# Raw scores in pairs, a stage's last values one step later, and three small VectorE steps in other forms

## The reference

```python
x = L0_attn_x                                   # 8 x 256 x 256, fp32
xn = _layernorm(x, axis=-1)
s = _L0_attn_ref(xn, ...)                       # latent attention, 16 heads, rotary part
g = _silu(_L0_ffn_ref(xn, ...))                 # attention block, then experts
x = x + s * g
...
# latent attention
c_q = x @ w_dq.T;  c_kv = x @ w_dkv.T
q = concat([c_q @ w_uq.T, rope(c_q @ w_qr.T)])  # per head 16 + 64
k = concat([c_kv @ w_uk.T, rope(x @ w_kr.T)])
out = softmax(q k^T * SCALE + causal mask) v;   s = out @ w_out.T
...
# the other branch
xn = _rmsnorm(x, w_ln1);  h = causal_attention(xn, 16 heads of 16)
x = residual + h @ Wo.T;  xn = _rmsnorm(x, w_ln2)
logits = xn @ Wr.T;  top 2 of 8 experts, softmax of the two
y = sum over experts of weight * (silu(Wg x) * (Wu x)) @ Wd
```

## Time and profile before

| what | us |
|---|---|
| median of 3 runs (809.0 to 813.9) | 810.94 |
| profiled execution | 808.98 |
| its span | 807.2 |
| TensorE busy in the span | 726.7 (90%) |
| VectorE busy | 551.0 (68%) |
| ScalarE busy | 429.0 (53%) |
| GpSimd busy | 387.9 (48%) |

### The profile page before, as it was taken

The page is one execution under the profiler, slowest core; times in us unless marked ns, Lnnn a source line. Parts: engine busy times, 40 slices in busy tenths (PEclk is TensorE's granted clock), DMA queues, the critical chain, the costliest instruction groups (busy, mean ns, idle before and its releaser), DMA issues.

```text
span 807.2 us, 17047 instructions
## 1 busy us (share of the span) xinstructions
PE 726.7 (90%) x5968; PEld 651.0 (81%) x5968; DVE 551.0 (68%) x1925; ACT 429.0 (53%) x895; POOL 387.9 (48%) x489
## 2 busy tenths in 40 slices
PE   4869999999999999999999999894799999999970
PEld 3858978978988987887888887572699999999970
DVE  3876567687587586586586596425488888888844
ACT  2434364365365365355355445451487777887752
POOL 3642452354453453463563464253455666556640
PEclk9978999999999999999999999777799999999995
DMA  9492663573473474384284186431889999999736
GB/s 293 109 177 48 92 152 74 78 163 77 64 159 83 64 151 103 50 161 107 40 159 107 43 159 160 140 104 30 234 204 240 230 230 229 262 275 254 170 36 217
DMA packets 81416, 115.54 MB, mean 143 GB/s; under 512 B 17475, under 2 KB 57667, under 8 KB 81283
## 3 DMA queue, kind: packets, MB, share of 16 engines
q1 hardware_dynamic: 70612, 101.74, 53.0%
q0 software_dynamic: 9856, 12.13, 8.5%
q10 hardware_dynamic: 864, 0.60, 0.3%
HBM read 70.06 MB, written 23.46 MB: 116 GB/s over the span
## 4 chain that ended last, share of the span: by engine, by line
PE 69%; DVE 12%; DMA 6%; issue 4%; ACT 4%; SPq 4%; POOL 2%; DVEq 0%; POOLq 0%; ACTq 0%
PE ps L703 63%; DVE ex L1572 2%; ACT ex L1299 2%; DVE stg L1571 2%; DVE ps L1631 2%; DMA qt<-stg 2%; PE ps L739 2%; SPq L446 2%; PE ps L1097 1%; DVE ps L1628 1%; DMA ln<-in_w_ln 1%; POOL stg L607 1%; PE ps L748 1%; SPq L458 1%; SPq L402 1%
## 5 line engine op out<-in xcount | busy, mean ns | idle before, releaser
L647 POOL TENSOR_SCALAR_AFFINE_SELECT ex<-ex 128x256 f32<-128x256 f32 x256 | 102.9, 407 | 169.8 <-ACT ex L1299 157.7
L1299 ACT ACTIVATE ex<-ps 128x384 f32<-128x384 f32 x240 | 115.8, 490 | 122.3 <-PE ps L703 118.5
L703 PE MATMUL ps<-qt,kt 81*128 81x128 f32 (+2 forms) x768 | 165.5, 330 | 4.2 <-issue 2.0
L1628 DVE CUSTOM_DVE_ANT_0 ps<-ps,mask 128x128 f32<-128x128 f32 x256 | 78.1, 305 | 74.3 <-PE ps L703 72.6
L703 PEld LDWEIGHTS ps<-qt,kt 81*128 81x128 f32 (+1 forms) x768 | 111.1, 197 | 15.8 <-issue 7.9
L607 POOL TENSOR_TENSOR stg<-stg,ex 128x512 f32<-128x512 f32 x64 | 82.5, 1291 | 80.2 <-DVE ex L1572 78.3
L1631 DVE CUSTOM_DVE_ANT_0 ps<-ps,mask 128x256 f32<-128x256 f32 x256 | 119.1, 465 | 0.0
L690 POOL DMA_INDIRECT expert_rows<-yo,slot_of x46 | 75.4, 1639 | 82.6 <-ACT yo L1419 63.1
L1456 DVE TENSOR_TENSOR wel<-raw,weh 128x768 fp32r<-128x768 f32 x92 | 87.7, 956 | 18.3 <-ACT weh L1150 18.3
L703 PE MATMUL ps<-xth,wh 128*128 128x256 f32 x384 | 78.9, 286 | 2.0 <-issue 2.0
L1571 DVE TENSOR_TENSOR stg<-ps,cos_t 128x512 f32<-128x512 f32 x64 | 44.1, 689 | 52.8 <-PE ps L703 45.8
(11 more groups left out here) (157 smaller groups left out, 1682.1 us busy)
## 6 DMA issues: line engine op xcount, KB each, us to landing
raw<-in_w_experts SPq DMA_DIRECT2D x92, 384.0 KB, 4.5
qt<-stg SPq DMA_DIRECT2D x64, 128.0 KB, 4.0
kt<-stg SPq DMA_DIRECT2D x64, 128.0 KB, 3.8
multi_heads<-stg SPq DMA_DIRECT2D x64, 128.0 KB, 2.4
qt<-multi_heads SPq DMA_DIRECT2D x32, 192.0 KB, 3.6
kt<-multi_heads SPq DMA_DIRECT2D x32, 128.0 KB, 3.4
qt<-stg SPq DMA_DIRECT2D x8, 256.0 KB, 4.6
kt<-stg SPq DMA_DIRECT2D x8, 256.0 KB, 6.1
```

The lines of the kernel that those rows point to most:

```text
L647: nc.gpsimd.affine_select(a, a, [[0, 2], [1, P]], ALU.is_ge, zero, 0, -1).then_inc(exm, 1)
L703: return nc.tensor.matmul(o, a, m, start=start, stop=stop, skip_group_check=True, **k)
L1299: nc.scalar.activation(ex[:, h % (2 * G), :], ps[4 + h % 2][:, P:4 * P], ACT.Exp, scale=scale).then_inc(ex_, 1)
L1628: nc.vector.tensor_tensor_reduce(out=o[:, 0:P], in0=o[:, 0:P], in1=mask2[:, 1, :], scale=-1.0, scalar=-2.0 * BIG, op0=ALU.add, op1=ALU.min ...
```

## The change

It has four parts. In T1 the raw heads are issued two at a time: heads h+1 and h+2 behind transposed head h, for h = 1, 3, ... 13, and none behind even heads. In T2 likewise: (4, 5) behind head 1, (6, 7) behind 3, (8, 9) behind 5, (10, 11) behind 7, (12, 13) behind 10, (14, 15) behind 12. T2's `values(3)` moves behind the next batch's first two raw heads, in the last batch too. Three small VectorE steps become two-tensor instructions that read the same tensor twice and take the larger of two equal numbers or of x + c and x.

```diff
@@ heads
-                    if h in ahead:
-                        max_head(ahead[h])
+                    for n in ahead.get(h, ()):
+                        max_head(n)
@@ stage_t1
-                             {h: h + 2 for h in range(H - 2)}, lambda: None, after)
+                             {h: (h + 1, h + 2) for h in range(1, H - 2, 2)}, lambda: None, after)
@@ stage_t2
-                ahead = {h: h + EARLY for h in range(8)} | {h: h + 3 for h in range(9, 13)}
-                heads(b, scores, st2, ex2, exm2, pv2, ov2, v2, before_h0, lambda: wait(pe, sd, b + 1), max_head, ahead,
-                      lambda: max_t1(b + 1), after)()
+                ahead = {h: (h + 3, h + 4) for h in range(1, 8, 2)} | {10: (12, 13), 12: (14, 15)}
+                return heads(b, scores, st2, ex2, exm2, pv2, ov2, v2, before_h0, lambda: wait(pe, sd, b + 1), max_head,
+                             ahead, lambda: max_t1(b + 1), after)
@@ batch (in the last batch alike)
                     max2(b)(0)
                     max2(b)(1)
                     if not first:
+                        values_before()
                         to_tokens()
...
-                    stage_t2(b, max1(b + 1), {2: project, 5: lambda: project_v2(b + 1)})
+                    return stage_t2(b, max1(b + 1), {2: project, 5: lambda: project_v2(b + 1)})
@@ stepped, plus_one, both
-                    nc.vector.tensor_scalar(step[:, :, :], step[:, :, :], 2.0 * P, None, ALU.add).then_inc(gst, 1)
+                    nc.vector.scalar_tensor_tensor(out=step[:, :, :], in0=step[:, :, :], scalar=2.0 * P, in1=step[:, :, :],
+                                                   op0=ALU.add, op1=ALU.max).then_inc(gst, 1)
-                    nc.vector.tensor_scalar(gsum[:, :], gexp[:, :], 1.0, None, ALU.add).then_inc(gst, 1)
+                    nc.vector.scalar_tensor_tensor(out=gsum[:, :], in0=gexp[:, :], scalar=1.0, in1=gexp[:, :],
+                                                   op0=ALU.add, op1=ALU.max).then_inc(gst, 1)
-                    copy(g[:, :, 0], gsum[:, :])
+                    nc.vector.tensor_tensor(g[:, :, 0], gsum[:, :], gsum[:, :], ALU.max)
```

More of the change, by code:

```diff
@@ L987, in p1_with_m1, with batch @@
                 stage_p1(b, after | {"mk": lambda: (head(0), head(1)), "q3": lambda: head(2), "k3": lambda: head(3)})
-            def batch(b, first, more):
+            def batch(b, first, more, values_before):
                 to_tokens = None
@@ L1081, in _ @@
             pe.wait_ge(s_c, 16 * 4)
-            batch(0, True, True)
+            values_left = batch(0, True, True, None)
             pe.wait_ge(wrd, 1)
             for b in range(1, last):
-                batch(b, False, True)
-            batch(last, False, False)
+                values_left = batch(b, False, True, values_left)
+            batch(last, False, False, values_left)
             def rows_transpose(blk):
```

## The result

The changed kernel takes 823.64 us (median of 4, 821.07 to 826.88), the kernel before 812.29 beside it: a ratio of 1.016 (95% interval 1.0129 to 1.0192), which is +13.0 us (10.5 to 15.6); the two medians by themselves are 11.4 apart. The forecast was +8.0 us, slower. The direction was right, the size was too small, and the median lies 0.14 us above the stated range.

What follows compares the result with a forecast made beforehand. The prediction took TensorE, busy 90% of the span, as what to watch, with its waits priced by stretch. T1's pairs 3.0, T2's boundaries 5.0 and small steps 0 made +8.0 us on 810.94: 818.9 us, range 806.0 to 823.5.

Steps and rivals of the forecast that it cites:

- Pairs in T1, first wait: T1, raw head 9: waits for maximum 7, which starts behind `kept`; `values(0)` 0.5 us later.
- Pairs in T1, the sum: T1, batches 1 to 6: six times 0.5 = +3.0 us; bounds 0 to 0.9 each, the upper if another pair waits.
- Pairs in T2: End of T2: `max_t1` and `values(2)` 0.50 us later behind maximum 15; nothing carried from the front.
- Values later: Batch boundary: mask wait hidden, ScalarE's copy uncovered, loads early enough; `to_tokens` +0.72 us including `max_t1`'s +0.50, seven boundaries +5.0.
- Small steps: P1 on VectorE: GpSimd holds the new two-tensor forms like the old ones; 0 us.
- The rival's price: P1: new forms escape GpSimd's hold, gaining 0.13 to 1.30 us each, -0.8 to -7.8 over six; chance 0.14, other gains over 4 us included.
- The sum: Whole kernel: 3.0 + 5.0 + 0 = +8.0 us, median 818.9 us.
- The range: Whole kernel: 806.0 to 823.5 us; upper end from T1 at 0.8 and a boundary at 1.1, 12.5 us in all.

Runs made afterwards that it cites:

- e14: Kernel before with T1's pairs alone, plus GpSimd's four scatters moved from behind masks 8 to 11 to behind 12 to 15; ratio 1.0075.
- e7: Kernel before with T1's pairs alone, plus VectorE's scaling moved from behind maximum 10 to behind 11; T1 21.92 us against 21.50, no ratio.
- e11: Kernel before with T2's pairs for raw heads 4 to 11 alone, raw heads 12 to 15 single where they were; ratio 1.0025.
- e1_small: Kernel before with the three small VectorE steps alone in their two-tensor forms; ratio 1.001.
- e6: Kernel before with L1747 cut into eight one-column instructions and P1's copy into two of one element; ratio 1.001 in its second run.
- e12_t1_spread: Kernel before with T1's pairs alone, plus `kept` moved behind maximum 7, statistics behind 9, scaling behind 11; ratio 1.0004.
- e13_no_hold: Kernel before with the small steps cut into one-element pieces, and the product of the two gates cut as well; ratio 1.0009.

## Why the prediction was right and wrong

- **Pairs in T1, first wait: right.** Forecast +0.5 behind `kept`; `values(0)` came at 10.81 against 10.31, with 0.25 of idle TensorE and a fresh weight load at raw head 9.
- **Pairs in T1, the sum: wrong, and this is the step that failed most.** "I take 0.5, as each of its terms has a row" priced one place. The upper bound named another pair that waits too, 0.9, but I neither looked for that pair nor priced it. It is raw head 13, and it costs 0.66 in batches 3 to 6. T1's mean loss of 0.94, over that bound, times 6 is 5.6, where 3.0 stood. The scaling, 0.63 in the kernel before, became twice as long because the new order put it beside GpSimd's scatter (e14), and it stood between the two maxima of a pair (e7). The very effect that I discussed for P1's small steps I didn't ask about for the other instructions whose time shifts.
- **Pairs in T2: right in size.** +0.50 forecast, +0.52 measured. "I carry nothing from there", said of the front, came out right for the full change, but not for the reason given: the maxima 10 and 11 come later by 0.46, and with them the cast of `qr`. It stays hidden because the late pair (12, 13) comes later still; with single raw heads there (e11) it is paid in full.
- **Values later: a step that failed too.** The uncovered copy was right: 1.36 from `values(3)` to `to_tokens` (251.28 to 252.64), with 0.51 of it idle. "Which I take as enough" was wrong, and the trace of the kernel before could have told it. The second of the loads in the earlier trace rows was issued at 242.10, and it landed 4.7 later (KB, us from issue to landing):

```profile
kt<-multi_heads SPq DMA_DIRECT2D x1, 64.0 KB, 4.7
```

  It was there at 246.75, 0.61 ahead of the raw heads at 247.36, and the prediction moved these to 246.72. A wait for these loads is one of the signs that the prediction itself named for being wrong. Besides, raw heads that start fresh take 0.66 up to `values(3)` instead of 0.57. A usual boundary cost 0.80 to 0.85, two with a wait for the load 0.97 and 1.27, and the average is 0.92 instead of 0.72; seven make 6.4 against 5.0.
- **Small steps: right.** Held before and after, 0 (e1_small). The Trainium skill's rule (SBUF — State Buffer, section Who interferes with whom), that a VectorE instruction with two SBUF inputs contends with a GpSimd instruction that reads SBUF, agrees with 1.15 and 1.28 in the changed kernel and with 1.14 in e6. The note that the prediction set against it (the Trainium skill, Advanced Engine Details and Errata, section Mode Summary) names only GpSimd and the Vector instructions that use both ports as blocking each other; to read it as letting two-tensor forms go free doesn't fit these numbers.
- **The rival's price: inside its bounds, near the lower one.** The bounds were 0.13 and 1.30 for each P1. Freed steps shorten P1 by 0.63 to 1.08, but the batch by at most 0.41, since T2 gives most of it back; the timed ratios show no gain at all.
- **The sum.** 5.6 + 6.4 = 12.0 by the stages, against 8.0; the timed ratio gives 13.0 (10.5 to 15.6). The profiled executions are 17.9 apart. Of the rest, 1.2 was there before the first pair was reached (`max_t1` of the first batch at 62.22 against 61.04), and 4.9 came behind the last boundary: from there to the end of the span 314.9 against 310.0, a stretch that takes 307.2 to 312.3 in the other kernels' profiles. The changed kernel's profiled execution is the longest of its four.
- **The range.** Its upper end took 0.8 for T1 and 1.1 for a boundary, 12.5 in all, and the stages' 12.0 on the 810.94 that the sum started from would be 822.9, inside it. Beside the changed kernel the one before took 812.29, 1.35 more. That the median lies just outside and not just inside is chance; that two terms were priced too low is not.

## What to carry to other kernels

When two buffers take turns, issuing their fills in pairs leaves no slack for anything else on the consumer between the two: price every other step of the consumer that lies inside a pair, not the one that is nearest. When an order changes, ask of each instruction that moves in time what runs beside it now; an instruction that was never held can become held. Count a transfer from its landing in the trace, not from its issue, before you move up what waits for it. A shorter step ahead of a transfer that ends last gives its time back at that transfer, so look for the next arrival before counting a gain.

## What the runs showed of the hardware

Two one-input scalings of 128x256 elements on VectorE took 0.61 together where only the last 0.14 of a mask of GpSimd's fell beside them (changed kernel, batch 1: mask 138.56 to 138.97, scaling from 138.83), and 0.63 where they came ahead of the scatter (kernel before, batch 3: 260.82, scatter from 261.12). They took 1.28 when the scatter (L630, 1.03) and a mask (0.42) were under way, and 0.99 beside masks alone (e12_t1_spread, batch 1: scalings from 137.72, masks from 137.03 to 138.56). Small steps of one element in each partition weren't held to the end of GpSimd's sums of 1.3: eight took 0.58, two 0.22.

In two batches of e13_no_hold T2's front, up to `values(0)`, took 10.7 us, in the others 8.8 to 9.1. The windows there (columns as above) show TensorE's granted clock fall right behind its waits at T2's start; the last row is T2's front in another batch, where it didn't fall:

```profile
291.96:295.06 3.10, 2.31 (x14) 1.62 (x13) 3.10 (x15) 2.20 (x6) 2.59 (x3) 1.00 0.92 214
295.06:297.83 2.77, 2.77 (x10) 2.21 (x9) 0.95 (x6) 0.30 (x1) 0.78 (x3) 0.55 0.83 154
355.62:366.00 10.38, 9.61 (x74) 7.92 (x72) 8.23 (x41) 6.14 (x13) 5.12 (x10) 1.00 0.62 145
```

At 0.55, near the lower of its two levels (1.2 and 2.4 GHz), the eight matmuls of `project` took 2.77 where they take 1.5 to 1.7. Why two batches and not the others isn't settled; without these two, e13's sum is 62.03, level with e6.
